# 128 of 496 field pairs computed with the batch on the partitions and summed over features by ScalarE

## What is computed

```python
e = stack([tbl_f[ids[:, f]] for f in range(32)], axis=1)      # 512 x 32 x 64
rows, cols = triu_indices(32, k=1)                            # 496 pairs
pij = einsum('bpe,dpe,bpd->bp', e[:, rows], kernel, e[:, cols])
z = pij @ W.T + b                                             # 512 x 256
h = maximum(concatenate([z, dense_ctx], axis=1) @ W_top1 + b_top1, 0)
h = maximum(h @ W_top2 + b_top2, 0)
y = h @ W_top3
```

## Time and profile before

| what | value |
|---|---|
| median of 3 runs | 256.03 us (255.77 to 256.83) |
| the profiled execution | 255.97 us |
| its span, first to last instruction | 254.2 us |
| busy: TensorE / VectorE / ScalarE / GpSimd | 96% / 72% / 20% / 54% |
| mean granted TensorE clock | 0.993 |
| moved by DMA | 16.38 MB, 64 GB/s mean |

### The profile page before, as it was taken

How to read it: one execution, slowest core, us unless ns; L and a number is a source line. 1 busy time by engine, 2 the same in 40 slices (tenths; PEclk the granted TensorE clock), 3 DMA queues, 4 the chain that set the end, 5 groups by cost and what they waited for, 6 DMA issues and landing times.

```text
span 254.2 us, 3686 instructions
## 1 busy us (share of the span) xinstructions
PE 243.8 (96%) x1378; PEld 93.8 (37%) x1378; DVE 183.6 (72%) x205; ACT 50.5 (20%) x86; POOL 136.9 (54%) x197
## 2 busy tenths in 40 slices
PE   7778799999999999999999999999999999999996
PEld 3443454333332333333323333333333323333474
DVE  1999996867778687887768788788778768870130
ACT  3768677111110102010100200100100100001121
POOL 5766988888888888878888878700000000000000
PEclk9799999999999999999999999999999999999999
DMA  6294322333323333333333331182000000000000
GB/s 168 57 279 114 83 60 73 82 85 81 76 77 78 86 84 75 77 77 83 83 75 83 72 84 34 21 274 49 0 1 3 0 0 3 0 0 0 0 3 0
DMA packets 11028, 16.38 MB, mean 64 GB/s; under 512 B 5166, under 2 KB 5810, under 8 KB 11010
## 3 DMA queue, kind: packets, MB, share of 16 engines
q1 hardware_dynamic: 7768, 12.97, 18.0%
q0 software_dynamic: 3072, 3.15, 6.8%
q10 hardware_dynamic: 170, 0.03, 0.1%
HBM read 16.13 MB, written 0.00 MB: 63 GB/s over the span
## 4 chain that ended last, share of the span: by engine, by line
PE 91%; ACT 3%; issue 3%; DVE 2%; DVEq 0%
PE t_ps L351 43%; PE sum_ps L372 23%; PE sum_ps L322 5%; PE tp_ps L322 3%; PE t_ps L412 3%; PE tp_ps L334 3%; ACT distance L460 2%; PE t_ps L355 2%; PE t_ps L359 2%; PE tp_ps L379 2%; PE sum_ps L295 1%; PE t_ps L421 1%; PE t_ps L379 1%; PE t_ps L352 1%; ACT own_sb L486 1%
## 5 line engine op out<-in xcount | busy, mean ns | idle before, releaser
L556 DVE TENSOR_TENSOR prod<-t_ps,x_sb 128x1024 f32<-128x1024 f32 x120 | 139.3, 1218 | 33.4 <-PE t_ps L352 32.8
L351 PE MATMUL t_ps<-x_sb,k_sb 64*128 64x512 f32 x240 | 113.4, 606 | 0.4 <-ACT own_sb L486 0.4
L352 PE MATMUL t_ps<-x_sb,k_sb 64*128 64x512 f32 x240 | 113.5, 607 | 0.0
L280 POOL DMA_INDIRECT gathered<-in_tbl,ids_sb x96 | 94.7, 987 | 26.8 <-issue 13.0
L351 PEld LDWEIGHTS t_ps<-x_sb,k_sb 64*128 64x128 f32 x240 | 41.4, 186 | 63.1 <-issue 37.6
L372 PE MATMUL sum_ps<-prod,sel_sb 128*32 128x512 f32 x496 | 59.6, 598 | 0.0
L287 POOL MEMSET rest_sb<- 128x380 f32 x96 | 42.0, 438 | 0.1
L352 PEld LDWEIGHTS t_ps<-x_sb,k_sb 64*128 64x128 f32 x240 | 41.4, 186 | 0.0
L482 ACT COPY x_sb<-tp_ps 128x512 f32<-128x512 f32 x14 | 8.2, 586 | 107.1 <-PE tp_ps L334 104.2
L372 PEld LDWEIGHTS sum_ps<-prod,sel_sb 128*32 128x32 f32 x496 | 12.9, 109 | 42.3 <-issue 21.3
L543 DVE TENSOR_SCALAR pair_sums<-ids_bc,iota_sb 125x512 bf16<-125x512 f16 x57 | 24.3, 488 | 2.5 <-ACT ids_bc L444 2.1
(11 more groups left out here) (56 smaller groups left out, 117.5 us busy)
## 6 DMA issues: line engine op xcount, KB each, us to landing
k_sb<-in_kern SPq DMA_DIRECT2D x112, 64.0 KB, 2.1
gathered<-in_tbl,ids_sb POOLq DMA_INDIRECT x96, 2.6
k_sb<-in_tbl SPq DMA_DIRECT2D x5, 280.0 KB
k_sb<-in_kern SPq DMA_DIRECT2D x4, 256.0 KB, 4.0
w_sb<-in_w SPq DMA_DIRECT2D x2, 512.0 KB, 5.0
k_sb<-in_tbl SPq DMA_DIRECT2D x3, 224.0 KB
w_pairs_sb<-in_w_pairs SPq DMA_DIRECT2D x1, 512.0 KB, 3.4
ctx_sb<-in_ctx_rows SPq DMA_DIRECT2D x1, 192.0 KB, 5.5
```

The lines of the kernel that those rows point to most:

```text
L280: pool.indirect_dma_start(gathered[:, n % G_RING, t, f * EMB:(f + 1) * EMB], None, tables[field], bass.IndirectOffsetOnAxis(ap=ids_sb[:, t ...
L351: pe.matmul(t[:, 0, :], k_sb[low, k, :], x_sb[low, a, :], start=True, stop=True)
L352: pe.matmul(t[:, 1, :], k_sb[high, k, :], x_sb[high, a, :], start=True, stop=True).then_inc(t_ready, 1)
L556: dve.tensor_tensor(prod[:, g % PROD_RING], t_ps[:, g % T_RING], q, ALU.mult).then_inc(prod_ready, 1)
```

## The change

Eight chunks (`FAR`) are paired with four (`NEAR`, chunks 4 to 7) in another way: these 32 chunk pairs, 128 of the 496 field pairs, leave the groups, of which 92 remain. For each far chunk and each 128 samples one **side unit** has the samples stationary (`x_sb`, 64x128) and four weight blocks moving (512 columns), on both halves of the array, so that the samples are on the partitions of `t_ps`. VectorE multiplies by the four near chunks as gathered, before any transpose. ScalarE sums each of the 16 stretches of 64 columns by an activation that also writes out the sum over its columns (`accum_out`). The 32 side units stand in the plan between groups 15 and 86. When all are summed, four transposes turn `side_sums` into window 0 of `pair_sums`. The chunks 4 to 7 stay in `gathered` for good, and the other chunks share the four remaining slots; `LEAD` becomes 5.

```diff
-GROUP = []
+NEAR = [4, 5, 6, 7]
+FAR = [0, 1, 8, 9, 10, 11, 12, 13]
+SIDE_TILES = 8 * len(FAR)
+SIDE_GROUPS = SIDE_TILES // 2
+SIDE_UNITS = BT * len(FAR)
...
+MAIN = []
 for c in range(CHUNKS):
-    across = [(c, False, [[(i, 2 * c), (i, 2 * c + 1)] for i in (2 * a, 2 * a + 1)]) for a in range(c)]
+    across = [(c, False, [[(i, 2 * c), (i, 2 * c + 1)] for i in (2 * a, 2 * a + 1)]) for a in range(c) if not is_side(c, a)]
...
+LEAD = 5
+SIDE_AT = [15 + 71 * m // (SIDE_UNITS - 1) for m in range(SIDE_UNITS)]
+SIDE = [(c, t) for c in FAR for t in range(BT)]
...
+        steps.append(("group", g))
+        while side < SIDE_UNITS and SIDE_AT[side] <= g:
+            steps.append(("side", side))
+            side += 1
+        if g == GROUPS - 2:
+            steps.append(("side sums", 0))
...
-REDUCES = NT // COLS
+REDUCES = 2 * GROUPS // COLS
...
-G_RING = 8
-LEAD = 3
+G_RING = len(NEAR) + 4
+SIDE_RING = 3
...
+def gathered_slot(n):
+
+    return n if n < len(NEAR) else len(NEAR) + (n - len(NEAR)) % (G_RING - len(NEAR))
...
                 if n >= G_RING:
-                    pool.wait_ge(filled, n - G_RING + ONE_HOTS + 1)
+                    pool.wait_ge(filled, n - (G_RING - len(NEAR)) + ONE_HOTS + 1)
...
+            def side_products(m):
+
+                c, quarter = SIDE[m]
+                u = UNITS.index(("side", m))
+                k = SIDE_BLOCK_OF[c]
+                if quarter == 0:
+                    weights_in(k, len(NEAR))
+                    pe.wait_ge(x_ready, 2 * (c + 1))
+                pe.wait_ge(prod_ready, u - T_RING + 1)
+                t = t_ps[:, u % T_RING]
+                cols = slice(quarter * P, (quarter + 1) * P)
+                low, high = slice(0, EMB), slice(EMB, P)
+                pe.matmul(t[:, 0, :], x_sb[low, c, cols], k_sb[low, k:k + len(NEAR), :].rearrange("p g m -> p (g m)"),
+                          start=True, stop=True)
+                pe.matmul(t[:, 1, :], x_sb[high, c, cols], k_sb[high, k:k + len(NEAR), :].rearrange("p g m -> p (g m)"),
+                          start=True, stop=True).then_inc(t_ready, 1)
+
+            def turn_side_sums():
+                pe.wait_ge(side_summed, SIDE_UNITS)
+                pe.wait_ge(x_ready, 2 * CHUNKS)
+                for t in range(BT):
+                    mm = pe.transpose(tp_ps[:, t * P:(t + 1) * P], side_sums[:, t, :], ident_sb[:])
+                mm.then_inc(side_turned, 1)
...
+            def sum_side(m):
+
+                c, t = SIDE[m]
+                k = FAR.index(c)
+                act.wait_ge(prod_ready, UNITS.index(("side", m)) + 1)
+                for n in range(16):
+                    part = side_prod[:, m % SIDE_RING, n // 8, n % 8 * EMB:(n % 8 + 1) * EMB]
+                    one = act.activation(part, part, ACT.Copy, accum_out=side_sums[:, t, 16 * k + n:16 * k + n + 1])
+                one.then_inc(side_summed, 1)
...
+            for u, (kind, g) in enumerate(UNITS):
+                dve.wait_ge(t_ready, u + 1)
+                if kind == "side":
+                    t = SIDE[g][1]
+                    if g >= SIDE_RING:
+                        dve.wait_ge(side_summed, g - SIDE_RING + 1)
+                    q = gathered[:, 0:len(NEAR), t, :].rearrange("p (o c) n -> p o c n", o=1)
+                    dve.tensor_tensor(side_prod[:, g % SIDE_RING].rearrange("p s (c n) -> p s c n", c=len(NEAR)),
+                                      t_ps[:, u % T_RING].rearrange("p s (c n) -> p s c n", c=len(NEAR)),
+                                      q.broadcast_to([P, 2, len(NEAR), P]), ALU.mult).then_inc(prod_ready, 1)
+                    continue
```

More of the change, by code:

```diff
@@ L41, with is_side, side_tile @@
 OH_RING = 8
-GROUP = []
+NEAR = [4, 5, 6, 7]
[3 more added lines that the diff above has]
+SIDE_UNITS = BT * len(FAR)
+def is_side(c, a):
+    return c in FAR and a in NEAR or c in NEAR and a in FAR
+def side_tile(k, s, n):
+    return 4 * (8 * (k % 2) + 4 * s + n) + k // 2
+side_tiles = {side_tile(k, s, n): [(2 * c + s, 2 * near), (2 * c + s, 2 * near + 1)]
+              for k, c in enumerate(FAR) for s in range(2) for n, near in enumerate(NEAR)}
@@ L51 @@
[L51 to L60, removed]
+    at = (1 - len(MAIN)) % RUN
+    MAIN += across[:at] + within + across[at:]
+GROUPS = len(MAIN)
+GROUP += MAIN
+NT = 2 * len(GROUP)
+WITHIN = [g for g in range(GROUPS) if MAIN[g][1]]
@@ new lines, with plan @@
+FIRST_GROUP = [min(g for g in range(GROUPS) if MAIN[g][0] == c) if c else 0 for c in range(CHUNKS)]
+LEAD = 5
+SIDE_AT = [15 + 71 * m // (SIDE_UNITS - 1) for m in range(SIDE_UNITS)]
+SIDE = [(c, t) for c in FAR for t in range(BT)]
+def plan():
+    steps, chunks, side = [], 0, 0
+    for g in range(GROUPS):
+        while chunks < CHUNKS and (chunks < max(2, ONE_HOTS) or g >= FIRST_GROUP[chunks] - min(LEAD, (chunks - 1) // 2)):
+            steps.append(("fill", chunks))
+            chunks += 1
+        steps.append(("group", g))
[4 more added lines that the diff above has]
+            steps.append(("side sums", 0))
+    return steps
@@ new lines @@
+STEPS = plan()
+UNITS = [step for step in STEPS if step[0] in ("group", "side")]
+UNIT_OF_GROUP = [UNITS.index(("group", g)) for g in range(GROUPS)]
+BLOCK, BLOCK_OF, SIDE_BLOCK_OF = [], [], {}
+for kind, n in UNITS:
+    if kind == "side":
+        c, t = SIDE[n]
+        if t == 0:
+            SIDE_BLOCK_OF[c] = len(BLOCK)
+            BLOCK += [tuple((side_tile(FAR.index(c), s, k), (0, 1), 2 * c + s) for s in range(2)) for k in range(len(NEAR))]
+        continue
+    _, within, tiles = MAIN[n]
+    g = SIDE_GROUPS + n
@@ L99, in reduced_after @@
     return range(max(0, (g - RUN - 1) // 2), (g - 1) // 2) if g % RUN == 1 else range(0)
[L102 to L110, removed]
+def gathered_slot(n):
+    return n if n < len(NEAR) else len(NEAR) + (n - len(NEAR)) % (G_RING - len(NEAR))
 def build(nc, ids, ids_t, iota, pick, tables, kern, w_pairs, b_int, ctx_rows, w_ctx_rows, w1, b1, w2, b2, w3, ident, selector, out):
-    steps = plan()
+    steps = STEPS
     with ExitStack() as ctx:
@@ L172, in build @@
         ids_ps = [t_ps[0:V_ROWS, f // 2 % T_RING, f % 2, :] for f in range(2 * ONE_HOTS)]
[L173 to L175 removed]
+        last = len(UNITS) - 1
+        z_ps = [tp_ps[:], t_ps[:, (last - 2) % T_RING, 1, :]]
+        y_ps = t_ps[:, (last - 2) % T_RING, 0, 0:P]
+        h1_ps = [t_ps[:, u % T_RING, h, :] for u in (last - 1, last) for h in range(2)]
         h2_ps = [[bank[:, 0:HALF] for bank in banks] for banks in ((sum_ps, tp_ps), h1_ps[0:2])]
@@ L333, in turn, with weights_in @@
                 for t in range(BT):
-                    mm = pe.transpose(tp_ps[:, t * P:(t + 1) * P], gathered[:, n % G_RING, t], ident_sb[:])
+                    mm = pe.transpose(tp_ps[:, t * P:(t + 1) * P], gathered[:, gathered_slot(n), t], ident_sb[:])
                 mm.then_inc(filled, 1)
+            def weights_in(k, blocks):
+                for s in range(SLICES):
+                    if k <= s * KS < k + blocks:
+                        pe.wait_ge(k_in[s], 16 * (2 if s < PIECES_FROM else PIECES))
@@ L337, in products @@
+            def turn_side_sums():
[4 more added lines that the diff above has]
+                mm.then_inc(side_turned, 1)
             def products(g):
-                c, within, tiles = GROUP[g]
+                c, within, tiles = MAIN[g]
                 k = BLOCK_OF[g]
-                for s in range(SLICES):
-                    if k <= s * KS < k + 1 + within:
-                        pe.wait_ge(k_in[s], 16 * (2 if s < PIECES_FROM else PIECES))
@@ L390, in _ @@
                         turn(n)
+                elif kind == "side":
+                    side_products(n)
+                elif kind == "side sums":
+                    turn_side_sums()
                 else:
@@ L484, in _ @@
                     if n >= SET and n % SET == 0:
-                        act.wait_ge(prod_ready, WITHIN[n // SET - 1] + 1)
+                        act.wait_ge(prod_ready, UNIT_OF_GROUP[WITHIN[n // SET - 1]] + 1)
                     act.copy(own_sb[rows, n % SET // 2, :], from_ps[rows, :]).then_inc(x_ready, 1)
+                elif kind == "side":
+                    sum_side(n)
+                elif kind == "side sums":
+                    act.wait_ge(side_turned, 1)
+                    act.copy(pair_sums[:, 0, :], tp_ps[:]).then_inc(side_kept, 1)
                 else:
@@ L544, in _ @@
                                   iota_sb[:, PICK[f][1] + r:PICK[f][1] + r + 1], None, ALU.is_equal).then_inc(one_hot_ready, 1)
-            for g in range(GROUPS):
-                c, within, _ = GROUP[g]
-                dve.wait_ge(t_ready, g + 1)
+            for u, (kind, g) in enumerate(UNITS):
+                dve.wait_ge(t_ready, u + 1)
+                if kind == "side":
+                    t = SIDE[g][1]
[5 more added lines that the diff above has]
+                                      q.broadcast_to([P, 2, len(NEAR), P]), ALU.mult).then_inc(prod_ready, 1)
```

(2 more changed lines are left out.)

32 lines of the change are left out of this document (20 added, 12 removed).

## The result

| what | before | after |
|---|---|---|
| median of 6 runs each | 255.54 us (254.60 to 256.83) | 258.10 us (256.80 to 259.51) |
| span of the profiled execution | 254.2 us | 256.6 us |
| mean granted TensorE clock | 0.993 | 0.973 |

The ratio is 1.0096, interval [1.0063, 1.0129]: slower by 1%. The forecast was 255.0.

What follows compares the result with a forecast made beforehand. TensorE, busy 96%, was taken as the bound, then waits for gathers: last product 223.9 + 1.0 (VectorE) + 0.2 (ScalarE) = 225.1, + 27.9 tail + 1.8 outside the span = 254.8, with semaphores 255.0 us; range 252 to 287.

Steps and rivals of the forecast that it cites:

- Removed work: TensorE: 64 tiles of reductions gone, 16.4 us, reductions from 496 to 368 instructions; 0.59 us added; tail unchanged.
- The gathers hold most of the gain: Turns of chunks 9 to 11: TensorE waits for gathered rows, 14.0 of the 16.4 us.
- The clock falls in the waits: TensorE behind chunk 11's wait: half clock for 3.3 us costs 1.7 us, giving 256.7; rival, chance 0.25.
- I take 1.0: Longer product bursts at 0.86 against VectorE's 1.13 us, three PSUM slots: 0 to 2 us of wait, 1.0 taken.
- I take 0.2: TensorE's wait for ScalarE's side sums near the end: nothing to 1 us at 0.25 a sum, 0.2 taken.
- Sum of the terms: Last product at 223.9 plus 1.0 for VectorE and 0.2 for ScalarE: 225.1 us.
- ScalarE at 0.25 us a sum: ScalarE's side sums: 0.15 pitch plus 0.10 for writing out the sum, 4.0 us a unit.
- the rival, priced by the same sum: ScalarE becomes the bound above 0.25 us a sum: 273 us at 0.30, 292 at 0.35; chance 0.22.
- That chunk copies queued behind the sums can stop TensorE: Chunk and window copies queue behind ScalarE's sums; TensorE stops on them if ScalarE falls behind; no size given.

Runs made afterwards that it cites:

- the gathers at 1.44 us: Three gathers in flight, pause between gathers cut from 380 to 250 columns: 244.00 us on the changed kernel, 253.40 us on the kernel before.
- Half a multiply: Changed kernel with the side multiply over 512 of its 1024 columns, eight of sixteen sums reading zeros: 256.25 us, ratio 1.0003.
- the version that does not wait: Changed kernel with three gathers in flight instead of two and the pause between gathers cut from 380 to 160 columns: 241.22 us.

## Why the forecast was wrong

- **Removed work: right.** 368 reduction instructions, and the tail as long as before (256.6 - 228.8 = 27.8).
- **The gathers hold most of the gain: right.** The turn of chunk 8 was placed at 76.2 and came at 76.03; the waits for 9, 10 and 11 were placed at landings of 88.6, 101.0 and 114.5 and ended at 87.76, 101.16 and 113.39. Their sum was 9.7 and not 14.0, since the low clock behind chunk 9's wait, which I had left out of the arrival at chunk 10, took 2.8 us of the next wait, and chunk 11's rows came 1.1 us early. With the gathers at 1.44 us the kernel gains 14.1 us, the kernel before 1.8, by its start.
- **"The clock falls in the waits", a rival at 0.25: it happened.** It was priced at 1.7 us and measured 1.8 to 2.0. This is the first failed step: the sum counted the waits and put the clock behind them at nothing. By the Trainium skill, "TensorE: Matmul & The Clock Gate", section "HAM oscillation", a wait for DMA makes the next burst start at the low clock; this trace agrees behind the waits of 4.53 and 3.34 us and not behind the one of 1.82, where the turn's record is 0.63.
- **"I take 1.0" for VectorE's bursts: too small.** From 117.58 to 224.23, 14 runs take 106.65 us; counted are 14 x 5.48, 24 units of 0.86, four turns and two within-set groups, 102.0. The excess is 4.6. By the difference that the forecast used it is 4.1 to 4.2: in seven profiles with the lead of five, whole multiplies and the full clock behind chunk 11's turn, the last product ends 113.48 to 113.54 us after it, and 109.4 were counted. The forecast had 1.0 there, and 2 as the upper end. The average (6.5 of 7.0 us) hid that each run of six products meets VectorE's pitch of 1.13 with three slots, and that a single short wait costs 0.16 (the run of 6.50). This is the second failed step, and the larger. Half a multiply took 2.4 us of it away; for the rest the same cause is argued.
- **"I take 0.2" for ScalarE: it cost nothing**, as the stretches of 113.5 us with and without the sums show.
- **Sum of the terms:** 225.1 forecast - 1.1 (rows) + 1.9 (clock) + 2.9 (bursts and ScalarE, 4.1 where 1.2 stood) = 228.8. The measured end was 228.79. That it closes is no proof, since the 2.9 is what the other terms leave over.
- **ScalarE at 0.25 us a sum: right.** The record pair has a pitch of 0.24 (below), a unit 3.86 us; the rival, priced by the same sum, came out at 274.8, where the forecast put 273 for 0.30 a sum, with the luck told above: the low clock made up for what ScalarE did faster. That chunk copies queued behind the sums can stop TensorE was named too; with a lead of five they don't, with three they do.

ScalarE's timeline after:

```profile
113.11 0.24 ACT L570 ACTIVATE side_prod<-side_prod 128x64 f32<-128x64 f32 x1
113.26 0.19 ACT L570 ACTIVATION_READ_ACCUMULATOR side_prod<-side_prod 128x1 f32 x1
113.35 0.24 ACT L570 ACTIVATE side_prod<-side_prod 128x64 f32<-128x64 f32 x1
```

## What to carry to other kernels

When work is taken out ahead of a stream of transfers, place every consumer again against the landings before counting the gain: here 9.7 of 16 us of TensorE turned into waits, and a stream with three gathers in flight, one each 1.36 us instead of 1.55, gave them back. A wait that the change creates has a second price, the clock behind it. Compare a producer and a consumer by their longest burst against the slots between them, not by their averages.

## What the runs showed of the hardware

- A sum over columns written out by ScalarE is two records, 0.24 and 0.19 us, at a pitch of 0.15 + 0.09 us: the read costs 0.09.
- GpSimd's memset between gathers slows VectorE's 16-bit compare, the more the longer it is: on average a compare takes 373, 383, 397 and 488 ns with pauses of 60, 160, 250 and 380 columns, in one profile each; others lie within 10 ns. The median stays at 353 with 380 columns; some records go up to 907 ns. By the Trainium skill, "SBUF — State Buffer", section "Who interferes with whom", a `tensor_scalar` in a 2-port mode and GpSimd exclude each other at the shared port pair; the two rows of L543 above agree, though none says in which mode the compare ran.
- With three indirect gathers in flight one is issued each 1.36 us without harm; at 1.28 us the changed kernel loses 69 us and the kernel before 84, while VectorE and ScalarE stand still. What holds them stays open: no run tells possible causes apart.
- The landings of gathers differ by 1 to 2 us between executions (chunk 11's turn at 113.15 to 114.58 in five profiles with two in flight, the long pause and the lead of five). A kernel that waits for them spreads as much: 256.8 to 259.5, while the version that does not wait stays within 240.96 to 241.31.
